# Split K and Q: six block copies stored to DRAM, or three parts stored once and repeated by the loads

## The reference, cut to what matters

```
q  = (latents @ q_w + q_b).reshape(b, k_len, NH, DH)
kv = (h @ kv_w + kv_b).reshape(b, p + k_len, NH, DH, 2)
kmat, v = (kv[..., 0], kv[..., 1])
attn = jnp.einsum('bkhd,bnhd->bhkn', q, kmat) / DH
attn = jnp.where(full_mask[:, None, None, :], attn, -jnp.inf)
attn = jax.nn.softmax(attn.astype(jnp.float32), axis=-1)
attn_out = jnp.einsum('bhkn,bnhd->bkhd', attn, v).reshape(b, k_len, H)
```

## Time and profile before

| | |
|---|---|
| median of 3 runs | 530.73 us |
| the profiled execution | 525.83 us, its span 524.0 us |
| granted TensorE clock, mean | 0.935 |
| PE busy | 431.6 us, 82% of the span |
| DVE busy | 327.8 us, 63% |
| ACT busy | 213.0 us, 41% |
| POOL busy | 110.8 us, 21% |
| HBM written, read | 14.68 MB, 31.63 MB |

### The profile page before, as it was taken

The page is one execution under the profiler, slowest core; times in us unless marked ns, Lnnn a source line. Parts: engine busy times, 40 slices in busy tenths (PEclk is TensorE's granted clock), DMA queues, the critical chain, the costliest instruction groups (busy, mean ns, idle before and its releaser), DMA issues.

```text
span 524.0 us, 7006 instructions
## 1 busy us (share of the span) xinstructions
PE 431.6 (82%) x2628; PEld 259.9 (50%) x2628; DVE 327.8 (63%) x592; ACT 213.0 (41%) x409; POOL 110.8 (21%) x103
## 2 busy tenths in 40 slices
PE   4988788888899988979989979799999796850555
PEld 2752243434674434458644544585564484530334
DVE  1257756563427577955767798447698544389753
ACT  1440056557415435633424547336368441120202
POOL 7320041110000041300104101402054400045400
PEclk9996599999999989999998999999999998795779
DMA  7789966354001831300054023000421000250001
GB/s 258 252 278 345 346 198 186 121 181 123 1 0 29 195 82 38 86 1 1 1 129 114 6 56 90 13 1 1 120 63 41 2 0 0 61 120 0 0 0 41
DMA packets 24696, 46.91 MB, mean 90 GB/s; under 512 B 2484, under 2 KB 18772, under 8 KB 23256
## 3 DMA queue, kind: packets, MB, share of 16 engines
q1 hardware_dynamic: 23672, 44.94, 29.9%
q10 hardware_dynamic: 992, 1.54, 0.9%
HBM read 31.63 MB, written 14.68 MB: 88 GB/s over the span
## 4 chain that ended last, share of the span: by engine, by line
PE 60%; DVE 24%; ACT 7%; issue 4%; DMA 3%; POOL 1%; SPq 0%; DVEq 0%; ACTq 0%; POOLq 0%
DVE mx L932 10%; PE pW L414 10%; PE pO L473 8%; PE pST L456 7%; PE pMX L441 6%; PE pW L558 5%; PE pW L549 5%; DVE A L897 4%; PE pW L487 4%; ACT probs L678 4%; PE pW L500 3%; PE pW L586 3%; PE pW L422 2%; DMA A<-v_rows 1%; DMA Wkq<-w_kq 1%
## 5 line engine op out<-in xcount | busy, mean ns | idle before, releaser
L932 DVE TENSOR_REDUCE mx<-pMX 128x1 f32<-128x512 f32 (+1 forms) x192 | 122.6, 685 | 43.6 <-PE pMX L441 43.0
L678 ACT ACTIVATE probs<-pST 128x512 f32<-128x512 f32 x192 | 103.9, 597 | 50.3 <-PE pST L456 49.0
L441 PE MATMUL pMX<-Kst,Qst 97*128 97x512 bf16 (+1 forms) x256 | 72.6, 354 | 23.3 <-DVE mx L932 22.2
L473 PE MATMUL pO<-probs,Vn 128*32 128x256 f32 x768 | 62.5, 397 | 0.9 <-ACT probs L678 0.4
L456 PE MATMUL pST<-Qst,Kst 99*128 99x256 bf16 x384 | 59.4, 277 | 0.8 <-ACT probs L678 0.8
L441 PEld LDWEIGHTS pMX<-Kst,Qst 97*128 97x128 bf16 x256 | 20.9, 99 | 69.1 <-DVE mx L932 53.3
L897 DVE TENSOR_TENSOR_SCAN A<-four,COL,A 128x256 f32<-128x256 f32 x64 | 53.9, 904 | 0.0
L456 PEld LDWEIGHTS pST<-Qst,Kst 99*128 99x128 bf16 x384 | 32.3, 98 | 33.7 <-ACT probs L678 16.8
L487 PE MATMUL pW<-hT,Wkq 128*128 128x256 f32 (+1 forms) x96 | 34.6, 514 | 7.7 <-DMA Wkq<-w_kq 7.3
L549 PE MATMUL pW<-T,Wup 128*128 128x256 f32 x128 | 29.0, 381 | 1.8 <-DVE SX L1101 1.2
L487 PEld LDWEIGHTS pW<-hT,Wkq 128*128 128x128 f32 x96 | 20.0, 215 | 20.8 <-issue 8.0
(11 more groups left out here) (135 smaller groups left out, 591.6 us busy)
## 6 DMA issues: line engine op xcount, KB each, us to landing
Kst<-k_stack SPq DMA_DIRECT2D x16, 576.0 KB
A<-v_rows SPq DMA_DIRECT2D x8, 1024.0 KB, 9.2
k_stack<-A SPq DMA_DIRECT2D x8, 576.0 KB, 3.2
k_stack<-A SPq DMA_DIRECT2D x8, 384.0 KB, 2.9
Qst<-q_stack SPq DMA_DIRECT2D x16, 192.0 KB
hT<-hT SPq DMA_DIRECT2D x3, 768.0 KB, 4.9
q_stack<-A SPq DMA_DIRECT2D x16, 128.0 KB, 3.1
Wsq<-w_sq SPq DMA_DIRECT2D x1, 2048.0 KB, 14.0
```

The source lines that it names most:

```text
L441: last = mm(pMX[n % 2][:, at:at + hi - lo], Qst[s][0:R_MASK + 1, h, qt * P:(qt + 1) * P], Kst[s][0:R_MASK + 1, h, lo:hi], start=True, stop ...
L473: last = mm(pO[32 * j:32 * j + 32, 0:TQ], Vn[b % 2][:, at:at + 32], probs[(n + j // 2) % UNITS_P][:, j % 2, :], start=nt == 0, stop=nt == ...
L678: act_fn(probs[n % UNITS_P][:], pST[n % ST_BANKS][:], ACT.Exp, scale=1.0 / DH)\
L932: v.tensor_reduce(dst, src, AX.X, ALU.max).then_inc(max_done, 1)
```

## The change

The DRAM tensors hold three parts instead of six blocks. A chunk's part is stored once for K and once for Q: six transfers per chunk instead of seven, and half the bytes. The load of a stack makes the repetition: a source with a leading dimension of step 0 gives K's high part three times, K's middle part twice and the low part once; Q's rows come as high, middle and low, then high and middle, then high. A stack's load is seven transfers (with the mask's row) instead of three. PE's count for a stack follows (112 instead of 48).

```diff
-K_BLOCKS = ((0, 0, 3, 1), (1, 3, 5, 1), (2, 5, 6, 1))
-Q_BLOCKS = ((0, 0, 4, 3), (0, 5, 6, 1), (1, 1, 5, 3), (2, 2, 3, 1))
-SPILLS = C * (len(K_BLOCKS) + len(Q_BLOCKS))
+PARTS = 3
+K_BLOCKS = ((0, 1, 0, 3), (1, 2, 3, 2), (2, 3, 5, 1))
+Q_BLOCKS = ((0, 3, 0, 1), (0, 2, 3, 1), (0, 1, 5, 1))
+SPILLS = C * 2 * PARTS
+STACK_IN = 16 * (len(K_BLOCKS) + len(Q_BLOCKS) + 1)
...
-        skd = nc.dram_tensor("k_stack", (B, NB, DH, NH, NK), BF16, kind="Internal").ap()
-        sqd = nc.dram_tensor("q_stack", (B, NB, DH, NH, TQ), BF16, kind="Internal").ap()
+        skd = nc.dram_tensor("k_stack", (B, PARTS, DH, NH, NK), BF16, kind="Internal").ap()
+        sqd = nc.dram_tensor("q_stack", (B, PARTS, DH, NH, TQ), BF16, kind="Internal").ap()
...
-                        for blocks, dst, lo, hi in ((K_BLOCKS, skd, 0, NK), (Q_BLOCKS, sqd, NK, NK + TQ)):
-                            for p_, first, end, by in blocks:
-                                if p_ == part:
-                                    n = len(range(first, end, by))
-                                    sp.dma_start(dst[b, first:end:by, :, c::C].rearrange("k d h n -> (d h) k n"),
-                                                 parts[:, part, c, lo:hi][:, None].to_broadcast([P, n, hi - lo]))\
-                                      .then_inc(kq_out, 16)
+                        for dst, lo, hi in ((skd, 0, NK), (sqd, NK, NK + TQ)):
+                            sp.dma_start(dst[b, part, :, c::C].rearrange("d h n -> (d h) n"), parts[:, part, c, lo:hi])\
+                              .then_inc(kq_out, 16)
...
-                    sp.dma_start(Kst[s][0:NB * DH], skd[b].rearrange("k d h n -> (k d) h n")[:, 4 * quad:4 * quad + 4])\
-                        .then_inc(stack_in[s], 16)
-                    sp.dma_start(Qst[s][0:NB * DH], sqd[b].rearrange("k d h n -> (k d) h n")[:, 4 * quad:4 * quad + 4])\
-                        .then_inc(stack_in[s], 16)
+                    for blocks, dst, src, n in ((K_BLOCKS, Kst[s], skd[b], NK), (Q_BLOCKS, Qst[s], sqd[b], TQ)):
+                        for first, end, at, times in blocks:
+                            part = src[first:end, :, 4 * quad:4 * quad + 4].rearrange("k d h n -> (k d) h n")
+                            rows = (end - first) * times * DH
+                            sp.dma_start(dst[at * DH:at * DH + rows],
+                                         part[None].to_broadcast([times, (end - first) * DH, 4, n]))\
+                              .then_inc(stack_in[s], 16)
...
-                        pe.wait_ge(stack_in[s], 48 * (g // STACKS + 1))
+                        pe.wait_ge(stack_in[s], STACK_IN * (g // STACKS + 1))
```

## The result

| | before | after |
|---|---|---|
| median (6 runs each) | 529.58 us | 576.90 us (573.72 to 581.31) |
| ratio after / before | | 1.1014, 95% interval 1.0956 to 1.1073 |
| profiled execution | 525.83 us, span 524.0 | 581.31 us, span 579.4 |
| granted TensorE clock, mean | 0.935 | 0.862 |
| PE's waits for a stack or the maxima's rows | none | 26.4 us |

The direction was forecast, the size was not: +47 us in place of +16. The time lies in the stated range, at its heavy end, but for another reason than the range had there.

What follows compares the result with a forecast made beforehand. The prediction took PE, then DVE, as the bound, with loads hidden; late narrow loads add 19.3 us, less 3 given back, so 16 us on 530.7 give 547 us, range 538 to 560 (8 in 10: 534 to 578).

Steps and rivals of the forecast that it cites:

- heavy end: Rival: in narrow K loads a row costs 0.35 us or more, delays add up; 560 to 580 us, chance 0.15.
- the load's fan-out: Stack loads: K's high part uses only 3 DMA engines and its middle part 2; a load takes 12.4 us, not 5.1.
- Loads spread: Rival: the repeated K source still spreads over 16 engines and every distance holds; 530.7 us, no difference, chance 0.08.
- faster: Rival: loads use 16 engines and the halved stores help in the saturated slices between 13 and 65 us; 529.3 us, chance 0.05.
- Mostly covered: Rival: K's high and middle transfers fall on different engines, so a load takes 8.1 us; 532 to 538 us, chance 0.12.
- The price of a row: Stack loads: a 6144 B K row costs 0.27 us on an engine; 27 extra rows make 7.3 us (6.8 to 10).
- The walk: Stack loads followed in time order: late at stacks 0, 3, 14 and maxima's rows behind stacks 11 and 15; 19.3 us.
- The weights' term: Ahead of stack 3's load: the queued 4096 KB of weights hold each DMA engine for 10.8 us.
- ACT's wait for batch 1's stores: Before stack 3: it passes at about 73 us, a few us late, and is counted within stack 3's 5.9 us.
- PE's clock can move either way: TensorE's granted clock after PE idles: it may keep or lose the grant; counted as nothing.
- I take 3 us off: Sum of PE's stalls: part is given back where other engines have run ahead, 3 us (between none and half).

Runs made afterwards that it cites:

- experiment 1: The changed kernel (parts stored once), but K's repetition loaded by single 16-row transfers, ten transfers per stack: 529.34 us, ratio 1.0116 to the kernel before.
- experiment 2: The kernel before's six stored blocks, but each stack loaded by the changed kernel's seven transfers with K's repeated narrow loads: 582.68 us, ratio 1.109.
- experiment 4: The changed kernel with 24 unread products on PE ahead of its waits for stacks and maxima's rows: 559.58 us, ratio 1.0741 to the kernel before.
- the control (5): The kernel with parts stored once and wide single-copy loads, plus 24 unread PE products where nothing is waited for: 547.36 us, ratio 1.0346.
- experiment 6: The kernel before with PE made to wait ahead of stack 3 for 20 small POOL products, no transfer touched: 544.89 us against 529.7, ratio 1.0287.
- experiment 11: The kernel before with 14, 5 and 1 unread products filling three PE pauses of the last 60 us: 525.92 us against 529.7, ratio 0.9959.
- experiment 10: Six blocks stored and narrow seven-transfer loads, but the three and two engines read distinct copies of K's parts: 577.37 us, ratio 1.0996 to the kernel before.
- experiment 3: The changed kernel with Q's parts repeated by the load in place of K's, same seven transfers and bytes: 534.47 us, ratio 1.0227 to the kernel before.

## Why the prediction was right and wrong

**What bounds the kernel, and that the load's fan-out decides: right.** The 2948 packets came out exactly; experiments 1 and 2 put the whole loss on the narrow loads. "Loads spread" and "faster" fell. "Mostly covered" fell with the stages that follow one another (shares 0.19, 0.12, 0.07): the transfers share their engines, as was assumed.

**The price of a row: right in sum, which is partly luck.** 0.27 us was taken, since few engines would disturb each other less than 16 do; the trace has 0.31 to 0.33 in the three-engine stage and 0.24 to 0.25 in the two-engine stage, the same 9 us for 32 rows. The single-engine stage behind them was missing, and with it up to 2 us of a load's length. The heavy end's reason (rows at 0.35 or more throughout) did not come true, although its time did.

**The walk: its five places right, two more late, the sum a quarter too small.** Forecast and measured: stack 0, 4.4 and 3.7; stack 2, 0 and 2.7; stack 3, 5.9 and 5.7; stack 6, 0 and 1.0; maxima's rows 1.9 and 2.4; stack 14, 3.3 and 4.9; maxima's rows 3.8 and 6.0. Together 19.3 and 26.4. The later ones are low because a load took 14 us there, not 12.4. The margins of stack 2 and 6 were under 1 us in the walk and should have been counted as lost. (The weights' term is 10.5 us by its own numbers, not 10.8, which takes 0.3 off stack 3; stack 0's load was issued 1.1 us earlier, forecast 0.7.) ACT's wait for batch 1's stores, taken as part of stack 3's, was 14.9 us long but held PE for 1.3.

**The step that failed: "PE's clock can move either way: an idle PE before a busy stretch may keep or lose the grant; I leave it at nothing", with "I take 3 us off" for time given back.** Nothing was given back; in the profiled pair 29.0 us came on top of the waits, while the time at the lower clock rose from some 68 to 160 us. Of the 47 us between the medians experiment 4 brought 17.3 back without touching a transfer, by filling the pauses; the control (5) shows that the fillers don't lift the clock without pauses, and experiment 6 has a loss of the same kind behind a pause alone (5.1 us in its trace). The remaining 30 us are about what the waits last. The kernel before showed it already: in its window 465 to 490 PE is busy for 4.1 of 25 us and the clock is 0.60 (the windows of experiment 11). I had read the clock as going either way.

The Trainium skill, "DMA: Bandwidth & Descriptors", section "Rules for kernel authors", was right on a repetition outermost: 3 copies gave a share of 0.19 and 2 copies 0.12 (3/16 = 0.19, 2/16 = 0.13), and the 2948 packets say the same.

**Still open.** Why three engines move some 18 to 20 GB/s each and two 24 to 26 (not the shared row, experiment 10). The 29.0 us in the profiled execution is not divided further between the lower clock and other things; experiment 4's 17.3 is an estimate of the clock's part, perhaps a low one, since 7.5 us of waits were left unfilled. Why a low stretch lasts 14 us in one run and 31 in another, and what holds the clock down at 46 to 68 us in the kernel before, no run shows.

## What to carry to other kernels

Look at the outermost count of both sides of a transfer: a repetition written as a leading dimension of 3 sends everything through 3 DMA engines, and the time is the rows on the busiest engine, counted with all transfers that share it and all that stands behind them in the queue. If bytes are to be repeated by the load, issue the copies singly (experiment 1, not told from before by its median) or repeat the small operand (experiment 3, some 2% slower); neither was faster than storing six blocks. Price a new stall of the critical engine at more than its length where TensorE is that engine: here a pause of 8.8 us put the program back by 13.9, and 26.4 us of waits came with 47 of loss.

## What the runs showed of the hardware that was not expected

- The granted clock falls in a pause of PE and stays low for long while PE works again: 0.50 for 20.4 us around a pause of 8.8 us (experiment 6), for 30.7 us beginning in a wait of 5.7 us (after). Products that nobody reads, put into the pauses, held it at 1.00 in the second case (experiment 4).
- Three DMA engines move little more than two: 60 against 49 GB/s in stack 10's load, and a single one 26, while 16 move 276 in the best slice of a stack's load.
